# TensorE's order inside an attention step: scores in two halves and the fold in two halves, around the transposes of the probabilities

## The reference, cut to what matters

```python
h = table[x]                                        # (128, 128, 128)
dots = einsum('bhid,bhjd->bhij', q, k) * scale      # q, k from layernorm(h)
dots = where(eye, MASK_VAL, dots)
dots = einsum('bhij,hg->bgij', dots, mix_pre)       # heads mixed before the softmax
attn = softmax(dots, axis=-1)
attn = einsum('bhij,hg->bgij', attn, mix_post)      # and after it
out  = einsum('bhij,bhjd->bhid', attn, v)
h = h + out @ Wout + bout
h = h + ffn(layernorm(h))                           # two routed banks, top 1, and a shared one
```

## Time and profile before

| What | Value |
|---|---|
| median of three runs | 1666.71 us |
| span of the profiled execution | 1659.7 us |
| TensorE busy over the span | 1495.3 us, 90% |
| VectorE, ScalarE, GpSimd busy | 67%, 69%, 68% |
| attention's steady part | 160 to 1075 us of the span |
| scores taken up in 300 to 1000 us | 94 steps, 7.45 us each |

### The profile page before, as it was taken

How to read it: one execution, slowest core, us unless ns; L and a number is a source line. 1 busy time by engine, 2 the same in 40 slices (tenths; PEclk the granted TensorE clock), 3 DMA queues, 4 the chain that set the end, 5 groups by cost and what they waited for, 6 DMA issues and landing times. The chain is left out here.

```text
span 1659.7 us, 37390 instructions
## 1 busy us (share of the span) xinstructions
PE 1495.3 (90%) x11183; PEld 1377.3 (83%) x11183; DVE 1119.0 (67%) x2864; ACT 1149.3 (69%) x3478; POOL 1129.5 (68%) x1105
## 2 busy tenths in 40 slices
PE   4306999999999999999999999987999988879999
PEld 2105999999989989989989999877999988879999
DVE  8957778878878777877878887752332444456555
ACT  3416988888888888888888888853555544445554
POOL 8835556787878878878878786656700767766665
PEclk8659999999999999999999999998999999989999
DMA  3332220000000000000000000002443555533333
GB/s 132 133 111 94 105 90 15 28 27 27 18 19 19 17 18 16 14 15 14 15 15 15 14 15 7 3 5 62 110 114 106 135 137 141 130 77 87 86 87 84
DMA packets 112855, 97.75 MB, mean 59 GB/s; under 512 B 26417, under 2 KB 98285, under 8 KB 112676
## 3 DMA queue, kind: packets, MB, share of 16 engines
q1 hardware_dynamic: 90896, 58.18, 11.4%
q0 software_dynamic: 20480, 31.01, 8.3%
q10 hardware_dynamic: 1300, 6.40, 1.0%
HBM read 53.96 MB, written 52.54 MB: 64 GB/s over the span
## 5 line engine op out<-in xcount | busy, mean ns | idle before, releaser
L774 ACT ACTIVATE expd<-masked,nmax 128x128 f32<-128x128 f32 x1024 | 395.9, 393 | 0.0
L585 POOL TENSOR_TENSOR prob<-expd,rtotal 128x1024 f32<-128x1024 f32 x128 | 243.3, 1901 | 134.1 <-DVE rtotal L852 133.6
L869 DVE COPY_PREDICATED masked<-off_diag,ps_s 128x1024 f32<-128x1024 int32 x128 | 175.2, 1369 | 139.3 <-PE ps_s L672 139.3
L714 PE MATMUL ps_o<-u,probT 128*128 128x128 f32 x2048 | 249.1, 275 | 0.7 <-issue 0.7
L714 PEld LDWEIGHTS ps_o<-u,probT 128*128 128x128 f32 x2048 | 239.0, 191 | 0.9 <-issue 0.9
L1352 POOL DMA_INDIRECT fq_back<-answered_sp,fq_back_i x128 | 122.5, 957 | 137.2 <-DVE fq_back_i L1313 103.0
L774 ACT ACTIVATION_READ_ACCUMULATOR expd<-masked,nmax 128x1 f32 x1024 | 196.9, 192 | 0.0
L783 ACT ACTIVATE u<-ps_ut 128x1024 f32<-128x1024 f32 x128 | 131.4, 1027 | 68.8 <-PE ps_ut L725 68.8
L797 ACT ACTIVATE probT<-ps_ut 128x1024 f32<-128x1024 f32 x128 | 131.6, 1028 | 51.3 <-PE ps_ut L680 44.7
L884 DVE TENSOR_TENSOR w_lo<-ps_w,w_hi 128x512 fp32r<-128x512 f32 x256 | 163.9, 680 | 4.4 <-ACT w_hi L804 4.4
L804 ACT ACTIVATE w_hi<-ps_w 128x512 fp32r<-128x512 f32 x256 | 146.2, 596 | 16.5 <-PE ps_w L702 10.0
(11 more groups left out here) (236 smaller groups left out, 4099.0 us busy)
## 6 DMA issues: line engine op xcount, KB each, us to landing
out<-sh_res SPq DMA_DIRECT2D x56, 128.0 KB, 2.3
h_sb<-in_L_tok_weight SPq DMA_DIRECT2D x10, 625.0 KB
table<-h_sb ACTq DMA_DIRECT2D x10, 625.0 KB
sent_sp<-zeros SPq DMA_DIRECT2D x8, 640.0 KB, 3.0
sent_fq<-zeros SPq DMA_DIRECT2D x8, 640.0 KB, 2.9
rows<-sent_sp SPq DMA_DIRECT2D x40, 128.0 KB, 3.1
answered_sp<-sp_res SPq DMA_DIRECT2D x40, 128.0 KB
rows<-sent_fq SPq DMA_DIRECT2D x40, 128.0 KB, 3.6
```

The source lines that it names most:

```text
L585: nc.gpsimd.tensor_tensor(prob[k % 2][:, :].rearrange("p (g j) -> p g j", g=H), expd[k % 2][:, :].rearrange("p (g j) -> p g j", g=H), rtot ...
L714: mm = nc.tensor.matmul(ps_o[:, 0:D], probT[k % 2][:, g * N:(g + 1) * N], u[k % 2][:, g * D:(g + 1) * D], start=(g == 0), stop=(g == H - 1))
L774: ins = nc.scalar.activation(expd[(k - 1) % 2][:, g * N:(g + 1) * N], masked[(k - 1) % 2][:, g * N:(g + 1) * N], ACT.Exp, bias=nmax[(k - 1 ...
L869: nc.vector.copy_predicated(masked[k % 2][:, :].rearrange("p (g j) -> p g j", g=H), off_diag[:, :].unsqueeze(1).to_broadcast([P, H, N]), p ...
```

## The change

Only TensorE's program is changed. The six score matmuls become two calls, `score(0)` for heads 0 to 3 and `score(1)` for heads 4 to 7, three matmuls each; the two quarters of the fold become two calls of `fold(q)`. The order in a step becomes: logits and counts as before, score(0), first quarter of the fold, transposes of the probabilities, in odd steps transposes of the input, second quarter of the fold, score(1), pv, u, x2 transposes as before. score(0) waits for two quarters of `w_lo`, score(1) for all four and raises `scored`. The wait for `xlo` stands ahead of the first quarter of the fold, and so ahead of the transposes. No instruction is added or taken away, and the programs of the other engines are the same.

```diff
                 if live(i, k):
+                def score(half):
                     m, b = k // 2, k % 2
-                    need(pe, S["copied"], tile(i, k))
-                    need(pe, S["w_lo"], group(i, k) * 4 + 4)
...
+                def fold(q):
+                    m = k // 2 + 1
+                    need(pe, S["w_lo"], group(i, 2 * m) * 4 + q - 1)
+                    for g in (2 * q, 2 * q + 1):
+                        o = ps_w[q % 2][:, (g % 2) * 256:(g % 2 + 1) * 256]
+                        M_hi, M_lo = (mats[n][:, g * D:(g + 1) * D] for n in ("M_hi", "M_lo"))
+                        nc.tensor.matmul(o, M_hi, xT_hi[:, m % 4, :], start=True, stop=False)
+                        nc.tensor.matmul(o, M_lo, xT_hi[:, m % 4, :], start=False, stop=False)
+                        mm = nc.tensor.matmul(o, M_hi, xT_lo[:, m % 4, :], start=False, stop=True)
+                    mm.then_inc(S["w_made"], 1)
+
+                if live(i, k):
+                    need(pe, S["copied"], tile(i, k))
+                    need(pe, S["w_lo"], group(i, k) * 4 + 2)
+                    score(0)
+
+                if live(i, 2 * (k // 2 + 1)):
+                    need(pe, S["xlo"], group(i, 2 * (k // 2 + 1)) + 1)
+                    fold(2 * (k % 2))
                 if live(i, k - 3):
...
                 if live(i, 2 * (k // 2 + 1)):
-                    m = k // 2 + 1
-                    need(pe, S["xlo"], group(i, 2 * m) + 1)
-                    for q in (2 * (k % 2), 2 * (k % 2) + 1):
...
+                    fold(2 * (k % 2) + 1)
+
+                if live(i, k):
+                    need(pe, S["w_lo"], group(i, k) * 4 + 4)
+                    score(1).then_inc(S["scored"], 1)
```

More of the change, by code:

```diff
@@ L661, in step @@
                     mm.then_inc(S["cum"], 1)
-                if live(i, k):
+                def score(half):
                     m, b = k // 2, k % 2
-                    need(pe, S["copied"], tile(i, k))
-                    need(pe, S["w_lo"], group(i, k) * 4 + 4)
                     cols = slice(b * N, (b + 1) * N)
@@ L670, in step @@
                         r = rhs[m % 2][:, b, :, :].rearrange("p g j -> p (g j)")
[L671 to L674, removed]
+                        mm = nc.tensor.matmul(ps_s[:, half * 512:(half + 1) * 512], lhs,
+                                              r[:, half * 512:(half + 1) * 512], start=(n == 0), stop=(n == 2))
+                    return mm
+                def fold(q):
[15 more added lines that the diff above has]
+                    fold(2 * (k % 2))
                 if live(i, k - 3):
```

## The result

The changed kernel takes 1871.41 us (median of four runs, 1863.32 to 1885.49) against 1666.99 before: 1.1246 times, 95% interval 1.1197 to 1.1295. The profiled execution took 1874.04 us, its span is 1872.3. The forecast was 1842 (1800 to 1890), slower at 0.97: direction and range held, and the measured time is 29 us above the forecast.

The account below looks back on a forecast made before the run. TensorE bounds the attention, its stream without gaps, so late hand-overs add up: 162 us, -2 for step 126, +12 for first steps, -5 for back-edges, together 167, giving 1834; with 8 for the clock 1842 us, range 1800 to 1890.

Parts of the forecast that it names:

- Matmuls, ScalarE, the fold: nothing: Attention step: same matmuls in another order, ScalarE's work at the same place, second fold quarter ready in time; no cost.
- cover ahead of the transposes: TensorE work before the probabilities' transposes, 1.47 us before, now 0.7 + 0.7: gain nothing, at most 11 us in all.
- `scored` 2.3 us later, against 3.19 us of stream: Scores end 2.3 us later in the step, leaving TensorE 3.19 instead of 5.48 us before asks of VectorE.
- the back-edges: Four idle pieces of TensorE before logits at the loop's back-edge, covered by the new logits waits: -5 us.
- (a): x2 transposes ending steps with k % 4 = 2 wait for x2: 2.29 us late in router steps, else 1.84.
- (b): Logits starting steps with k % 4 = 0 wait for h1: 1.75 us late behind router steps, else 1.45.
- (c): Start of steps with k % 4 = 2: counts wait 2.27 us for h1 (router), else fold 2.0 for xlo.
- (d): First w_lo of the previous step: needed 3.55 us against 3.89, not late; up to 0.1 with router pieces.
- The clock: 8 us: Attention's steady part: one in six of some 28 waits of 2.3 us brings a 1.2 GHz stretch, 1.7 us each.
- Rival 1: Clock falls behind many waits: 60 us at half of 70 waits, 1894 us; at all 1953; chance 0.12.
- Rival 2: Only part of the late hand-overs counts: 1780 us with two kinds, 1725 with only one; chance 0.10.
- rival 3: Not slower: the later copy merely shifts VectorE's phase and nothing is late, 1667 or 1659 us; chance 0.03.

Follow-up runs that it names:

- e1: Kernel before with only the fold halved around the transposes, scores whole at the step's start: 1814.10 us against 1814.29 before, 0.9996 times.
- e2: Kernel before with only the scores halved around the transposes, fold whole behind the second half: 1883.98 us against 1814.29 before, 1.0362 times.
- e3: Changed kernel with score(1) one place earlier, ahead of the second fold quarter: 1918.08 us against 1814.29 for the kernel before, 1.0584 times.
- e4: Changed kernel with score(1) later, behind pv: 2379.80 us against 1814.29 for the kernel before, 1.3108 times.
- e6: Changed kernel plus five matmuls on constants ahead of each late ask of TensorE: 1840.68 us, 1.1063 times the kernel before.
- e8: As e7, with VectorE's x2 block one place further ahead, before the reciprocal that releases GpSimd's multiplication: 1810.52 us, 1.0867 times the kernel before.
- e7: Changed kernel with VectorE's x2 block moved to just ahead of its copy of the scores: 1825.07 us, 1.0984 times the kernel before.

## Why the prediction was right, and where it was short

*What bounds the kernel, and that every wait adds.* Right. TensorE's stream had no gap before, and nothing gave back a wait.

*Matmuls, ScalarE, the fold: nothing.* Right for the change (e1). Of the cover ahead of the transposes I asked only what more of it could gain; e2 shows that it costs 35 us when it falls to 0.7 us. The change kept it at 1.4, so the sum didn't suffer.

*`scored` 2.3 us later, against 3.19 us of stream.* Right, and the step on which all hangs: e3 and e4 move only score(1), by one block each, and the waits follow, 0.63 less for 0.7 and 1.7 more for 1.7. The sum of these terms was 167; measured 161, less the 5 of the back-edges, 156. By places, with 0.16 added to each wait: (a) 50 us in 29, mean 1.73 against 2.07 foreseen. Part of the 0.34 is a misreading: the 0.14 between weight load and first matmul was no need of the hand-over, since TensorE was still busy with u until then. Where it waits, the matmul starts 0.01 behind its weight load (VectorE's x2, the weight load and the matmul of one step):

```profile
743.93 0.59 DVE L909 TENSOR_SCALAR x<-h_sb,mv,rstd 128x128 f32 x2
744.57 0.42 PEld L744 LDWEIGHTS ps_x<-ident,x 128*128 128x128 f32 x4 [2.32 <-DVE x L909]
744.58 0.66 PE L744 MATMUL ps_x<-ident,x 128*128 128x128 f32 x4 [1.89 <-DVE x L909]
```

Outside router steps it is too large by 0.22 more, because the x2 pair that I read in the earlier trace rows took 0.81 us, where the pair of the earlier trace rows took 0.59. (b) 46 in 29, 1.57 against 1.60. (c) with counts 31 in 14, 2.20 against 2.27; without 34 in 18, 1.92 against 2.0. (d) once. A slip in (b): 658.64 + 0.29 - 654.34 is 4.59, not 4.57, which is worth 0.3 us in the sum.

*The clock: 8 us.* This is the term that was mis-sized. It measured 45 in the profile, and e6 gives at least 37. The step that failed is "one in six" of "some 28 waits", 5 falls: there were 22. I let only the waits of 2.3 count, as long as those in the earlier trace rows, and took the rate from very few of them. Behind those 28 (the counts, and x2 in router steps) the clock fell 9 times, one in three; the other 13 falls lie behind waits to which I gave none. In e4, where four kinds of waits average 3.3 us, the same cost is 222 us.

*The total.* 156 + 45 is 201, and the medians differ by 204. In the run-up, 128 to 160 us, the clock is 0.71 now where it was 0.93, 7 us more. The spans of the two profiled executions differ by 213; some 5 us of that are not assigned. The waits came out 11 below my sum and the clock 37 above, so the forecast missed by less than the clock's error alone; that the two have opposite signs was luck.

*Rivals.* Rival 1 is what happened besides, by my own sign of it, the clock at 0.5 in more than ten stretches: there were over twenty. By its price (60 us for 35 falls, 1894 or more) it went a good half of the way. The Trainium skill, "TensorE: Matmul & The Clock Gate", section "A second HAM failure mode", says that short idles between groups of matmuls can be frequent enough for the clock to swing back and forth; the traces agree, with a mean of 0.96 here and 0.85 in e4. Rival 2 falls with the list of waits, which has all three hand-overs, and rival 3 with the same.

## What to carry to other kernels

Where one engine's stream has no gap, an order inside its step is judged by what stands between each signal it raises and the next thing it asks back, against the latency of the loop through the other engines; the idle time of those engines says nothing about that. Splitting a group so that its end comes later takes that distance away even though no instruction is added. When such waits come up often on TensorE, add the slow clock behind them to the price, and read it from the granted clock, not from the list of waits: 90 waits of 1.2 us on average brought one fall (e3), 90 of 1.8 us 22 and 29 (the change), 92 of 3.4 us, with 46 shorter ones, brought 90 (e4), the 0.16 included.

## What the runs showed of the hardware that I had not expected

- VectorE's tensor_scalar on 128 x 128 (f32 in SBUF) took 346 ns alone (e8) and stood still while GpSimd multiplied from SBUF to SBUF: two took 2.17 us, and the held one ended within 0.1 us of GpSimd (e7). The copy out of PSUM was not held: in the changed kernel it took 1.35 us, started at 728.40, beside the same multiplication from 728.36 on. The Trainium skill, "SBUF — State Buffer", section "SBUF: two separate sides", describes one pair of ports that the two engines lock in turn, for a whole instruction; these rows agree.

```profile
728.36 1.92 POOL L585 TENSOR_TENSOR prob<-expd,rtotal 128x1024 f32<-128x1024 f32 x1
```

- The clock falls behind single waits of 1.3 to 2.4 us in this stream, and not the same number of times in each execution: 22 and 29 times, 0.96 and 0.95 as means of the same program, 13 us apart. The length of the wait alone does not tell where: in e8, 24 of 26 falls lie behind the 29 waits for the logits (1.6 us on average), none behind the 14 before the counts (1.7). What sets it was not looked into.
- On the chip of the first four experiments the kernel before took 1814.29 us, on the others 1664 to 1667. Read from e1, which is as fast as the kernel before there: the attention's steady part was equal (909.30 busy in 915), what follows was not. Behind the last copy of the scores it took 741 us against 591; its last 520 us had TensorE at 425.04 us busy and a clock of 0.86, against 478.39 and 0.97 in the earlier trace rows. Why was not looked into. The change itself was not run on that chip; in e2, e3 and e4 the time behind the last copy is 741, 739 and 739 us, nearly that of e1, so their differences lie in the attention.
